# Row maxima of a cross-attention in seven tiles of 128 rows, with a second stack of keys

## What is computed

```python
def _mha(xk, xv, xq, Wk, Wv, Wq, Wo, bo, masked):
    K = jnp.einsum('bse,hed->bhsd', xk, Wk)      # 16 heads of 8
    V = jnp.einsum('bse,hed->bhsd', xv, Wv)
    Q = jnp.einsum('bqe,hed->bhqd', xq, Wq)
    scores = jnp.einsum('bhqd,bhkd->bhqk', Q, K)
    att = jax.nn.softmax(scores / jnp.sqrt(sk), axis=-1)
    out = jnp.einsum('bhqk,bhkd->bhqd', att, V)
    return jax.nn.relu(out @ Wo + bo)
c = _mha(context_seq, context_seq, a, Wk2, Wv2, Wq2, Wo2, bo2, masked=False)
```

## Time and profile before

| | us |
|---|---|
| median of 3 runs (3326.21 to 3329.63) | 3328.9 |
| the profiled execution | 3331.2 |
| its span in the trace | 3329.2 |
| in it, stage L2b: first units to last scores | 2144 to 2832 |
| PE busy over the whole span | 3075.9 (92%) |
| DVE / ACT / POOL busy | 2249.9 / 1742.0 / 1876.2 |

### The profile page before, as it was taken

One profiled execution on the slowest core, in us unless ns is written; L12 is line 12 of the kernel. 1 busy time (PEld: TensorE's weight loads), 2 busy tenths in 40 slices (PEclk: granted clock), 3 DMA queues, 4 the chain that ended last, 5 costly groups with the idle time before them and its releaser, 6 DMA issues. The chain is left out here.

```text
span 3329.2 us, 74410 instructions
## 1 busy us (share of the span) xinstructions
PE 3075.9 (92%) x30182; PEld 2128.4 (64%) x30182; DVE 2249.9 (68%) x4146; ACT 1742.0 (52%) x2864; POOL 1876.2 (56%) x1054
## 2 busy tenths in 40 slices
PE   7979998999999999999988999799999999569969
PEld 5654546777777777777775777555555555336644
DVE  4555557777777777777754444479999997663455
ACT  3534334666666656666653454356666666225545
POOL 0004546777777777777753212168888888224327
PEclk8989997999999999999998998789999999789989
DMA  7641016666666676666731666633333331505500
GB/s 136 142 118 37 1 26 117 135 133 139 138 143 133 134 139 140 136 134 134 138 73 49 233 244 227 193 85 95 95 95 96 95 95 50 93 1 112 122 1 12
DMA packets 607380, 367.70 MB, mean 110 GB/s; under 512 B 462933, under 2 KB 566626, under 8 KB 606786
## 3 DMA queue, kind: packets, MB, share of 16 engines
q1 hardware_dynamic: 607042, 362.96, 47.2%
HBM read 174.41 MB, written 75.24 MB: 75 GB/s over the span
## 5 line engine op out<-in xcount | busy, mean ns | idle before, releaser
L1742 POOL TENSOR_TENSOR L_plo<-L_p,L_phi 128x1500 bf16<-128x1500 f32 x224 | 659.1, 2942 | 293.9 <-DVE L_phi L1819 293.9
L1699 ACT COPY L_ptlo<-L_lt 128x1536 bf16<-128x1536 bf16 x224 | 322.1, 1438 | 406.6 <-PE L_lt L1623 406.6
L2121 ACT ACTIVATE L2b_p<-L2b_score 125x448 f32<-125x448 f32 x768 | 378.7, 541 | 275.2 <-PE L2b_score L2034 273.1
L1637 PE MATMUL L_acc<-L_chi,L_pthi 125*128 125x128 bf16 x2688 | 462.1, 219 | 0.0
L1639 PE MATMUL L_acc<-L_chi,L_ptlo 125*128 125x128 bf16 x2688 | 461.4, 219 | 0.0
L1638 PE MATMUL L_acc<-L_clo,L_pthi 125*128 125x128 bf16 x2688 | 461.2, 219 | 0.0
L1808 DVE TENSOR_SCALAR_CACHE_REDUCE L_p<-L_score,L_cols 128x1500 f32<-128x1500 f32 x224 | 395.4, 1765 | 83.7 <-PE L_score L1615 83.5
L1819 DVE CAST L_phi<-L_p 128x1500 bf16<-128x1500 f32 x224 | 298.1, 1331 | 164.6 <-ACT L_p L1693 163.7
L1693 ACT ACTIVATE L_p<-L_p,L_least 128x1500 f32<-128x1500 f32 x224 | 346.6, 1547 | 66.9 <-DVE L_p L1808 63.1
L2164 POOL TENSOR_TENSOR L2b_psum<-L2b_p 125x896 f32<-125x896 f32 x128 | 266.7, 2084 | 133.0 <-ACT L2b_p L2121 130.6
L2191 DVE TENSOR_REDUCE L2b_max<-L2b_m 112x1 f32<-112x1000 f32 x256 | 300.6, 1195 | 17.9 <-PE L2b_m L2015 10.2
(11 more groups left out here) (644 smaller groups left out, 6844.9 us busy)
## 6 DMA issues: line engine op xcount, KB each, us to landing
L2b_kst<-L_keys SPq DMA_DIRECT2D x96, 375.0 KB, 5.6
L_ct<-L_ct SPq DMA_DIRECT2D x32, 768.0 KB
L2a_ct<-L_ct SPq DMA_DIRECT2D x32, 768.0 KB, 15.1
L_ctx<-dram_ctx SPq DMA_DIRECT2D x32, 750.0 KB
L_keys<-L2a_kout SPq DMA_DIRECT2D x32, 750.0 KB, 8.0
L_values<-L2a_vout SPq DMA_DIRECT2D x32, 750.0 KB
L2b_vin<-L_values SPq DMA_DIRECT2D x32, 750.0 KB
L0x_ctx<-dram_ctx SPq DMA_DIRECT2D x32, 672.0 KB
```

Of the source, the lines that this page charges most:

```text
L1637: pe.matmul(acc, w_hi[0:KP, t, :], v_hi[0:KP, t, :], start=(t == 0), stop=False)
L1699: act.copy(pt_lo[g % 2][:, :, :], lt_ps[:, 0:KT * 128].rearrange("p (t q) -> p t q", t=KT)).then_inc(lo_read, 1)
L1742: pool.tensor_tensor(p_lo[g % 2][:, :, 0:KP], probs[g % RP][:, :].rearrange("q (t k) -> q t k", t=KT), p_hi[g % 2][:, :, 0:KP], ALU.subtra ...
L2121: act.activation(probs[t % RP][:, half * 2 * GW:(half + 1) * 2 * GW], score_ps[half][0:KP, 0:2 * GW], ACT.Exp).then_inc(exp_done, 1)
```

## The change

- The 896 rows are cut in P = 7 tiles of 128 rows. That makes 21 products of 500 columns in MAXU = 11 units, the last with one product (500 columns) alone.
- A tile of 128 rows no longer ends where a group of four heads (224 rows) ends. Tiles 1, 3 and 5 straddle two groups. For them a second stack `k_mix` holds, in each of the three blocks of 32 rows, rows 0 to 15 from the group above and rows 16 to 31 from the group below, three such mixed groups in all. It is loaded by six more DMAs of 16 rows x 3 x 3000 B (144 KB each, 864 KB in all) per batch, placed between the key and the value transfers; the unit with k = 1 waits for them.
- The negated maxima are made, turned and written once per batch instead of twice: one "negmax" unit in slot 29, a DVE write of seven rows of 896. `k_stack` and `q_top` have 103 rows instead of 100. All scores of a batch now wait for that one write.
- The units stand in slots 28, 31, 34, 2, 4, 7, 11, 14, 18, 21, 24. `max3` is double; `q_top`, `probs` and `p_sum` are allocated in the outer space.

```diff
-    G, R, RK = H // 4, 100, 3
+    G, R, RK = H // 4, 103, 3
...
+        for r0, w in ((0, 0), (32, 1), (64, 0)):
+            keys = k_dram[n, :, w, :].rearrange("(g r) n -> r g n", g=G)
+            sp.dma_start(k_mix[n % RK][r0:r0 + 16, :, :], keys[0:16, 1:G, :]).then_inc(mix_loaded[n % RK], 16)
+            sp.dma_start(k_mix[n % RK][r0 + 16:r0 + 32, :, :], keys[16:32, 0:G - 1, :]
+                         ).then_inc(mix_loaded[n % RK], 16)
         sp.dma_start(v_in[n % RK][:, :, :], v_dram[n].rearrange("k (t d) -> k t d", d=D)
...
-    P, PW = H // 2, 2 * S
-    R = 100
+    P, PW = HQ // 128, 128
+    R = 96 + P
...
-    MAXSLOT = (28, 31, 34, 2, 3, 7, 10, 14, 18, 20, 23, 25)
+    MAXSLOT = (28, 31, 34, 2, 4, 7, 11, 14, 18, 21, 24)
...
-    PLAN += [(1, "query", 0, "u", 2), (12, "out", 0, "u", -1), (21, "negmax", 0, "u", 1), (30, "negmax", 1, "u", 1)]
+    PLAN += [(1, "query", 0, "u", 2), (12, "out", 0, "u", -1), (29, "negmax", 0, "u", 1)]
...
+                        if k == 1:
+                            pe.wait_ge(mix_loaded[n % RK], 96 * (n // RK + 1))
                         for p, j, at in parts(k):
+                            keys = k_mix if p % 2 else k_stack
                             m = pe.matmul(ps[0:PW, at * 512:at * 512 + TK], q_top[n % RK][0:96, p * PW:(p + 1) * PW],
-                                          k_stack[n % RK][0:96, p // 2, third(j)], start=True, stop=True)
+                                          keys[n % RK][0:96, p // 2, third(j)], start=True, stop=True)
...
-                    if t == 0:
-                        pe.wait_ge(*freed("negmax", half, b))
+                    if s == 0:
+                        pe.wait_ge(*freed("negmax", 0, b))
```

More of the change, by code:

```diff
@@ L1882, in key_stacks @@
 def key_stacks(space, name, k_dram, v_dram):
-    G, R, RK = H // 4, 100, 3
+    G, R, RK = H // 4, 103, 3
     k_stack = [space.sb(f"{name}_kst{k}", [R, G, KEYS], BF16) for k in range(RK)]
+    k_mix = [space.sb(f"{name}_kmix{k}", [96, G - 1, KEYS], BF16) for k in range(RK)]
+    mix_loaded = [space.sem(f"{name}_mix_loaded{k}") for k in range(RK)]
     v_in = [space.sb(f"{name}_vin{k}", [KP, KT, D]) for k in range(RK)]
@@ L1888, in key_stacks @@
     v_loaded = [space.sem(f"{name}_v_loaded{k}") for k in range(RK)]
+    q_top = [space.sb(f"{name}_qst{k}", [R, HQ], BF16) for k in range(RK)]
+    probs = [space.sb(f"{name}_p{k}", [KP, HQ]) for k in range(6)]
+    p_sum = [space.sb(f"{name}_psum{k}", [KP, HQ]) for k in range(2)]
     pair_of_ones = float(np.uint32(0x3F803F80).view(np.float32))
@@ L1927, in narrow_heads_attention @@
         PROLOGUE.append(("max", n % MAXU, f"m{n % 2}", n // MAXU))
-        if n % 6 == 5 and n < MAXU:
-            PROLOGUE.append(("negmax", n // 6, "u", 0))
+        if n == MAXU - 1:
+            PROLOGUE.append(("negmax", 0, "u", 0))
     BUFS = ("u", "m0", "m1")
@@ L1941, in planned @@
     def planned(b):
-        return [(s, kind, k, f, b + d) for s, kind, k, f, d in PLAN if 0 <= b + d < B]
+        return [(s, kind, k, f"m{(MAXU * (b + d) + k) % 2}" if kind == "max" else f, b + d)
+                for s, kind, k, f, d in PLAN if 0 <= b + d < B]
     turn, used = {}, dict.fromkeys(BUFS, 0)
@@ L1954, in narrow_heads_attention @@
         q_parts = sp_.sb(f"{name}_qparts", [96, G * S], BF16)
-        q_top = [sp_.sb(f"{name}_qst{k}", [R, HQ], BF16) for k in range(RK)]
+        q_top, probs, p_sum = [stacks[k] for k in ("q_top", "probs", "p_sum")]
         v_one = sp_.sb(f"{name}_vone", [KP, 32])
-        probs = [sp_.sb(f"{name}_p{k}", [KP, HQ]) for k in range(RP)]
-        p_sum = [sp_.sb(f"{name}_psum{k}", [KP, HQ]) for k in range(2)]
-        max3 = sp_.sb(f"{name}_max3", [PW, P, 2])
-        negmax = [sp_.sb(f"{name}_negmax{k}", [PW, R]) for k in range(2)]
-        delta = sp_.sb(f"{name}_delta", [R, 4])
+        max3 = [sp_.sb(f"{name}_max3{k}", [PW, P, 2]) for k in range(2)]
+        negmax = sp_.sb(f"{name}_negmax", [PW, R])
+        delta = sp_.sb(f"{name}_delta", [R, P])
         pair = sp_.sb(f"{name}_pair", [128, 2, S])
@@ L2189, in unit @@
                         v = ps[0:PW, :].rearrange("p (i n) -> p i n", i=2)[:, :, 0:TK]
-                        if k % 3 < 2:
-                            dve.tensor_reduce(max3[:, p, 0:1], v, AX.XY, ALU.max).then_inc(free[f], 1)
-                        else:
-                            dve.tensor_reduce(max3[:, p:p + 2, 1], v, AX.X, ALU.max).then_inc(free[f], 1)
-                        if k % 6 == 5:
-                            half = k // 6
+                        if k == MAXU - 1:
+                            dve.tensor_reduce(max3[n % 2][:, p, 1:2], v[:, 0, :], AX.X, ALU.max).then_inc(free[f], 1)
+                        elif k % 3 < 2:
+                            dve.tensor_reduce(max3[n % 2][:, p, 0:1], v, AX.XY, ALU.max).then_inc(free[f], 1)
+                        else:
+                            dve.tensor_reduce(max3[n % 2][:, p:p + 2, 1], v, AX.X, ALU.max).then_inc(free[f], 1)
+                        if k == MAXU - 1:
                             dve.wait_ge(free[f], u + 1)
-                            dve.tensor_reduce(negmax[half][:, 96:R], max3[:, 4 * half:4 * half + 4, :], AX.X, ALU.max,
+                            dve.tensor_reduce(negmax[:, 96:R], max3[n % 2][:, :, :], AX.X, ALU.max,
                                               negate=True).then_inc(negmax_ready, 1)
@@ L2225, in divide @@
                     dve.tensor_tensor(heads[:, :], pair[:, 0, :], recip[:, :], ALU.mult).then_inc(heads_ready, 1)
-                for k in range(2):
-                    dve.memset(negmax[k][:, :], 0.0)
+                dve.memset(negmax[:, :], 0.0)
                 dve.memset(v_one[:, :], 1.0)
```

24 lines of the change are left out of this document (14 added, 10 removed).

## The result

| | before | after |
|---|---|---|
| median of 6 runs each | 3329.3 us (3326.2 to 3333.0) | 3312.3 us (3309.3 to 3316.3) |
| the profiled execution | 3331.2 us | 3309.7 us |
| its span | 3329.2 us | 3308.0 us |

The ratio is 0.9951 (95% interval 0.9941 to 0.9962): the changed kernel is 0.5% faster, 17.0 us in the medians, where 12 were forecast. Two executions in the experiments, one of the kernel before and one of it with the mixed loads, took 8.4 and 8.8 ms, and the ratios leave them out.

The account below looks back on a forecast made before the run. PE was taken to bound the loop. Loop -21.7, half-clock start of the loop -0.4 and stage start +10 sum to -12.1 us: 3319.1 on the profiled execution, 3317 us against the median; own range 3308 to 3325, with rivals 3308 to 3345.

Parts of the forecast that it names:

- PE is the bound, and products are worth their distance: Loop, PE: three fewer products and one turn of the maxima save 0.70 us a batch, -21.7 us over 31 batches.
- DVE and POOL stay behind: Loop: DVE falls to about 16.6 us a batch against a 19.9 us period; POOL's sum keeps about 0.4 us slack.
- rival 3: Loop: small waits eat 0.3 us a batch of the gain, giving 3327 us; chance 0.12.
- The single write: Loop, DVE: the one write takes 1.1 us and ends 1.3 us before the scores need it; cost 0.
- The mixed keys arrive in time: Loop loads: mixed keys take 6.5 us of the 7.7 us available before slot 31; cost 0.
- Rival 1: Mixed keys come too late in every batch, PE stops 0.9 us in slot 31, total +16, 3345 us; chance 0.24.
- Rival 2: Mixed keys load in 4.3 us whatever the rows, the start costs 5 us, total -17, 3312 us; chance 0.14.
- The start, to the first scores: Stage start: more loads in the queue delay batch 1's mixed keys and the first scores, +10 us (+5 to +14).
- the cold start of the loop: Start of the loop, still at half clock: the same work costs double, so -0.4 us more is saved.

Follow-up runs that it names:

- the slow write: The changed kernel with two more DVE operations of the size of the 7x896 write ahead of that write; 3345.5 us (one run).
- keys first: The changed kernel with keys and mixed keys of batches 0 and 1 loaded ahead of both batches' values at the start; ratio 0.9923 to the kernel before.

## Why the prediction was right, step by step

- **PE is the bound, and products are worth their distance.** Right. 0.74 us a batch came out where 0.70 stood. Its parts came out otherwise: three products 0.63, and nothing from the turn, now one of 0.19 (2498.22 to 2498.41, PE's timeline) where two of 0.10 were, instead of the 0.07 booked. The other 0.1 us is not at one place, and I leave it open.
- **DVE and POOL stay behind.** Right. DVE has 338 us of 400, 16.8 us a batch (16.6 forecast). POOL's sum was to have 0.4 us of slack; PE waited for it only at the very end of the stage (0.7 us in all), so rival 3 (0.3 us a batch in small waits) did not come.
- **The single write.** Right in all parts: 1.097 us (1.1 taken, 0.63 to 1.26 the bounds), and it ended 1.1 us ahead of the scores (1.3). The run with the slow write shows this slack and its price directly.

```profile
2499.03 1.10 DVE L2218 TENSOR_TENSOR L2b_qst<-L2b_u,L2b_delta 7x896 bf16<-7x896 f32 x1
```

```profile
2501.25 0.60 PE L2050 MATMUL L2b_score<-L2b_qst,L2b_kst 103*125 103x224 bf16 x4
```

- **The mixed keys arrive in time.** Right: 6.1 us (6.5 taken between 4.3 and 8.6), landing 14.1 us after the first issue (14 to 15), needed at 15.4 (15.4): the load issued at 2483.35 is first read at 2498.79. Reasoning from both ends gave a place between them, and which place was in part luck: that successive transfers go to different rows, the reason given, moves the six by 0.2 to 0.5 us in the two runs with other orders. An estimate by the rate of the Trainium skill's page "SBUF — State Buffer", section "Door 1: The DMA port swizzle", would have been 8.3 us; no run shows it.

```profile
2483.35 1.25 SPq L1898 DMA_DIRECT2D L2b_kst<-L_keys  x3
```

```profile
2498.79 0.59 PE L2031 MATMUL L2b_m<-L2b_kmix,L2b_qst 96*128 96x500 bf16 x2
```

- **Rival 1.** Its mechanism exists, and its price was too low. It counted a late key one for one; the run with the mixed keys last shows that a stop of 5 us or more costs another 2 at half clock. For a stop of 0.9 us, as rival 1 had it, the slow write speaks for one to one.
- **Rival 2's number.** The measured 3312.3 is rival 2's 3312, and its sum (-22.1 + 5) is nearly the one found below. Its mechanism was not there: the mixed keys took 6.1 us and not 4.3, and the first scores came 9.3 to 9.9 us later and not 5.
- **The start, to the first scores.** Right in sum: +10 forecast, 9.3 to 9.9 measured (10.7 in the trace's own time, at 2181.34), with the two waits for batch 1's transfers as described. The block began 6.9 us later in the trace's time and 6.1 from the last store (5 to 10). Its reason was half right: SP's long stall (13.98 us for the third load's keys, before 5.11) did not move into `first_stacks`. Ahead of the block it is the twelve issues that cost, 5.6 us, with 1.4 us of stall.
- **The term that was mis-sized is the cold start of the loop**, put at -0.4 us. The working let the start's cost stand until the end and took the half-clock stretch of the loop as equally long on both sides. It was shorter in both traces of the changed kernel (7.7 and 9.1 us after the first scores, where before had 17.8 and 14.8): 2.6 to 4.6 us come back within the first batch beyond the period's gain. With 4.5 to 6.0 us in place of 10 for what is left of the start, and 22.1 for the loop, the sum is -16.1 to -17.6 against -17.0 measured. Why the clock rose sooner stays open, and by the spread over executions part of this gain may be luck.
- **What the prediction did not ask** is whether the start had to cost anything. It took the order of the first loads as given; keys first, which moves no byte, takes most of that cost away (-26 us, as the kernel without mixed keys).

## What to carry to other kernels

Cost a new transfer twice: in the loop by when it is needed against when it lands (here 1.3 us to spare, and free), and at the start by everything that the same queue must carry ahead of the first data that anyone waits for. If the second is dear, reorder the first loads (what is needed first, for all early batches, ahead of what is needed late) before giving up the change. And look how long the stretch at half clock behind the start lasts before a delay of the start is booked in full: here about half of the delay came back against before, and almost none of it between the changed kernel and the one without mixed keys.
